# Decoder layer: project the raw transposed activations and apply the first layer norm to the products

## The reference, cut to what matters

```python
def _layernorm(x, axis=-1, eps=1e-05):
    m = jnp.mean(x, axis=axis, keepdims=True)
    v = jnp.var(x, axis=axis, keepdims=True)
    return (x - m) / jnp.sqrt(v + eps)

def _L0_attn_ref(x, Wqkv, bqkv, Wo, bo):          # d = 256
    qkv = jnp.einsum('bsc,cf->bsf', x, Wqkv) + bqkv
    q, k, v = ...
    attn = jax.nn.softmax(jnp.einsum('bqd,bkd->bqk', q, k) * scale, axis=-1)
    return jnp.einsum('bsd,dc->bsc', attn @ v, Wo) + bo

x = x + _L0_attn_ref(_layernorm(x), Wqkv, bqkv, Wo, bo)
x = x + fake_quant(_layernorm(x)) @ fake_quant(ctx)      # ctx (2, 1024, 1024)
x = x + _L0_ffn_ref(_layernorm(x), c1_w, c2_w, w1, w2t)  # picks 1 of 64 hidden units, 3584 in all
```

## Time and profile before

| | |
|---|---|
| median of 3 runs | 773.7 us (773.12 to 774.2) |
| the profiled execution | 773.81 us |
| its span in the profile | 772.0 us |
| instructions | 11300 |
| PE busy | 764.8 us, 99% |
| DVE busy | 606.9 us, 79% |
| POOL busy | 483.8 us, 63% |
| ACT busy | 242.4 us, 31% |

### The profile page before, as it was taken

One profiled execution on the slowest core, in us unless ns is written; L12 is line 12 of the kernel. 1 busy time (PEld: TensorE's weight loads), 2 busy tenths in 40 slices (PEclk: granted clock), 3 DMA queues, 4 the chain that ended last, 5 costly groups with the idle time before them and its releaser, 6 DMA issues.

```text
span 772.0 us, 11300 instructions
## 1 busy us (share of the span) xinstructions
PE 764.8 (99%) x3604; PEld 627.6 (81%) x3608; DVE 606.9 (79%) x963; ACT 242.4 (31%) x368; POOL 483.8 (63%) x306
## 2 busy tenths in 40 slices
PE   8999999999999999999999999999999999999998
PEld 7888887478888888888888888888888888888886
DVE  5887769997884878887878788788888887778864
ACT  5348668773321130312122221203031212222120
POOL 4887798766999974645636372636464563736360
PEclk9999999999999999999999999999999999999999
DMA  9436405400111121222222221212122222222114
GB/s 335 190 111 216 167 4 157 60 7 8 62 54 60 41 67 52 69 75 68 75 68 68 68 75 61 73 36 66 56 68 75 68 75 68 68 68 68 61 41 191
DMA packets 57319, 63.70 MB, mean 83 GB/s; under 512 B 39120, under 2 KB 41168, under 8 KB 57040
## 3 DMA queue, kind: packets, MB, share of 16 engines
q1 hardware_dynamic: 57152, 62.35, 25.9%
q10 hardware_dynamic: 144, 1.05, 0.3%
HBM read 50.79 MB, written 4.19 MB: 71 GB/s over the span
## 4 chain that ended last, share of the span: by engine, by line
PE 93%; DVE 4%; DMA 1%; ACT 1%; issue 1%; SPq 0%; DVEq 0%; ACTq 0%
PE bank L1881 13%; PE bank L1880 13%; PE bank L1882 13%; PE bank L1781 12%; PE bank L1782 12%; PE bank L1780 12%; PE bank L1589 4%; PE bank L1591 4%; PE bank L1590 4%; PE bank L1771 2%; DVE x L1267 1%; DMA x<-x_in 1%; PE bank L1750 1%; DVE xn L1248 1%; PE bank L1732 1%; PE bank L1605 1%
## 5 line engine op out<-in xcount | busy, mean ns | idle before, releaser
L1880 PE MATMUL bank<-w_hi,h_hi 128*128 128x512 f32 x448 | 175.2, 391 | 0.0
L1881 PE MATMUL bank<-w_lo,h_hi 128*128 128x512 f32 x448 | 175.0, 391 | 0.0
L1882 PE MATMUL bank<-w_hi,h_lo 128*128 128x512 f32 x448 | 174.3, 389 | 0.0
L1387 DVE TENSOR_TENSOR x<-bank,x 128x512 f32<-128x512 f32 x208 | 133.5, 685 | 48.9 <-PE bank L1882 48.8
L641 POOL TENSOR_TENSOR lo_r<-r,slot 128x512 fp32r<-128x512 f32 x52 | 68.1, 1311 | 141.0 <-ACT slot L880 141.0
L1882 PEld LDWEIGHTS bank<-w_hi,h_lo 128*128 128x128 f32 x448 | 84.1, 188 | 17.8
L1880 PEld LDWEIGHTS bank<-w_hi,h_hi 128*128 128x128 f32 x448 | 84.1, 188 | 17.2 <-POOL w_lo L646 0.2
L1881 PEld LDWEIGHTS bank<-w_lo,h_hi 128*128 128x128 f32 x448 | 84.4, 188 | 15.2
L1780 PE MATMUL bank<-xT_hi,slot 128*128 128x512 f32 x240 | 93.7, 390 | 0.0
L1781 PE MATMUL bank<-xT_lo,slot 128*128 128x512 f32 x240 | 93.4, 389 | 0.0
L1782 PE MATMUL bank<-xT_hi,lo_r 128*128 128x512 f32 x192 | 74.7, 389 | 0.0
(11 more groups left out here) (213 smaller groups left out, 1585.2 us busy)
## 6 DMA issues: line engine op xcount, KB each, us to landing
r<-w SPq DMA_DIRECT2D x56, 256.0 KB, 3.6
w_raw<-w SPq DMA_DIRECT2D x28, 512.0 KB, 4.0
x<-x_in SPq DMA_DIRECT2D x8, 512.0 KB, 10.3
ctx_raw<-ctx_in SPq DMA_DIRECT2D x8, 512.0 KB, 3.7
xn<-ctx_in SPq DMA_DIRECT2D x8, 512.0 KB, 4.3
out<-x SPq DMA_DIRECT2D x7, 512.0 KB, 2.6
W_raw<-wqkv SPq DMA_DIRECT2D x6, 512.0 KB, 11.0
xT_raw<-xT_in SPq DMA_DIRECT2D x1, 2048.0 KB, 19.8
```

Source lines behind the costliest of these rows:

```text
L1387: nc.vector.tensor_tensor(x[:, t, c], bank[unit_banks(g)[p]][:, :], x[:, t, c], ALU.add).then_inc(unit_added, 1)
L1880: nc.tensor.matmul(dst, h_hi[:, j, m], w2_hi[:, j, c], start=j == 0, stop=False)
L1881: nc.tensor.matmul(dst, h_hi[:, j, m], w2_lo[:, j, c], start=False, stop=False)
L1882: last = nc.tensor.matmul(dst, h_lo[:, j, m], w2_hi[:, j, c], start=False, stop=j == GJ - 1)
```

## The change

The raw transposed activations of both batches are loaded (xT_in is now of both), split and multiplied, and the norm is applied to the products. With r the scale and s the shift of a token, (x r + s) W = r (x W) + s (sum of W over channels). So:

- Q and K of batch 0 come first, as one product over eight slabs of 128 channels into four banks at once (`project_first_qk`), each chunk of one or two slabs as its loads land. The T1 jobs, the R jobs and ACT's norm of round 0 are gone. WARM is 18.
- DVE makes the lo part of the raw xT of batch 0 (`lo_xT0`, SBUF operands), POOL that of batch 1 (`lo_xT1`), and DVE sums the weight slabs one by one (`sum_W`, 7 steps of 512 columns, `sum_W_value`, 7 of 256). Each step waits for the one before. PE finishes the sum over partitions (`sum_weights`, within V(0,0)).
- PE spreads r and s of a batch into banks 7 and 6, ACT copies them to SBUF (`copy_rows`). DVE multiplies each Q bank by r (`scale_Q`) and adds s times the weight sum (`shift_Q`) before ACT's hi_Q. Each V half gets two steps of the same kind on DVE (`lo_V`) in the place of one addition for both.
- The loads are in another order, with one load issued by ACT. The first context load waits for V(0,1). POOL's add_bo runs behind the statistics of its tile and is spread among other work; the output bias has its own semaphore.

The diff, cut to its core:

```diff
-WARM = 44
+WARM = 18
+K_CHUNKS = [(0, 1), (1, 2), (2, 4), (4, 6), (6, 8)]
-    jobs = both("T1", 0) + both("T1", 1) + both("T1", 2) + [("V", 0, 0)] + both("T1", 3)
-    jobs += [("V", 0, 1), ("Q", 0, 0), ("R", 0), ("Q", 0, 1), ("R", 1), ("Q", 0, 2), ("Q", 0, 3), ("V", 1, 0)]
+    jobs = [("Q", 0, c) for c in range(4)] + [("V", 0, 0), ("V", 0, 1), ("V", 1, 0)]
...
 # SP
-            load_x(0, 1)
-            load_W(W_ORDER[0], 0, 1)
-            load_x(2, 3)
-            load_W(W_ORDER[1], 0, 1)
...
+            load_xT0(0)
+            load_xT0(1)
+            load_W(1)
+            load_xT0(2)
+            load_W(2)
+            load_x(0)
+            load_xT0(3)
+            load_W(3)
+            load_x(1)
+            load_xT0(4)
+            load_W(4)
+            load_x(2)
+            load_W(VALUE_CHUNK)
+            load_x(3)
+            load_W(VALUE_CHUNK + 1)
+            sp.dma_start(bqk_s[:, :], bqk).then_inc(bias_loaded, 16)
+            sp.dma_start(bv_b[:, :], bv.partition_broadcast(P)).then_inc(bias_loaded, 16)
+            load_xT1(0, 1)
+            sp.dma_start(bo_b[:, :], bo.partition_broadcast(P)).then_inc(bo_loaded, 16)
             load_x(4, 5)
+            load_xT1(2, 3)
...
+            load_x(6, 7)
-            sp.wait_ge(mm_done, nth("Q", 0, 3) + 1)
+            sp.wait_ge(mm_done, nth("V", 0, 1) + 1)
 # POOL
+            for c in range(VALUE_CHUNK + 2):
...
+                nc.gpsimd.tensor_tensor(w_part(W_lo, c), w_part(W_raw, c), w_part(W_hi, c).bitcast(F32),
+                                        ALU.subtract).then_inc(W_lo_done, 1)
+            lo_xT1(0, 1)
...
-            add_bo(0, 1, 2, 3)
-            lo_xT(0)
-            add_bo(4)
-            lo_xT(1)
-            add_bo(5)
+            add_bo(0)
+            lo_xT1(2, 3)
+            add_bo(1, 2, 3, 4)
             convert_ctx(0, 1)
+            add_bo(5)
+            convert_ctx(2, 3)
             add_bo(6)
-            convert_ctx(2, 3)
+            convert_ctx(4, 5)
             add_bo(7)
-            convert_ctx(4, 5, 6, 7)
+            convert_ctx(6, 7)
 # ACT
+            for c in range(VALUE_CHUNK):
+                hi_xT0(c)
+                if c > 0:
+                    hi_W(c)
+            hi_W(VALUE_CHUNK)
+            hi_W(VALUE_CHUNK + 1)
             roots(0, 0)
...
+            hi_xT1(0)
+            hi_W_ksum()
+            copy_rows(0)
+            for c in range(1, X1_CHUNKS):
+                hi_xT1(c)
+            for c in range(4):
+                hi_Q(0, c)
             hi_V(0, 0)
...
             hi_V(0, 1)
...
             scale_ctx(0)
             scale_ctx(1)
+            roots(0, 4)
...
+            copy_rows(1)
             for c in range(4):
                 hi_Q(1, c)
                 scale_ctx(2 * c + 7)
                 scale_ctx(2 * c + 8)
 # DVE
+            def scale_Q(b, c):
+                dve.wait_ge(mm_done, nth("Q", b, c) + 1)
+                dve.wait_ge(rows_copied, 2 * b + 1)
+                link(nc.vector.tensor_tensor(job_bank("Q", b, c)[:, :], job_bank("Q", b, c)[:, :], row_home[0][:, :],
+                                             ALU.mult))
+            def shift_Q(b, c):
+                dve.wait_ge(rows_copied, 2 * b + 2)
+                nc.vector.scalar_tensor_tensor(job_bank("Q", b, c)[:, :], row_home[1][:, :], wsum[:, c:c + 1],
+                                               job_bank("Q", b, c)[:, :], ALU.mult, ALU.add).then_inc(q_scaled, 1)
+            def add_slab(total, before, slab):
+                nc.vector.tensor_tensor(total, before, slab, ALU.add).then_inc(W_ksummed, 1)
+                ksums[0] += 1
+                dve.wait_ge(W_ksummed, ksums[0])
...
+            nc.vector.tensor_copy(w_part(W_hi, 0), w_part(W_raw, 0)).then_inc(W_hi0_done, 1)
+            lo_xT0(0)
+            lo_xT0(1)
+            sum_W(1)
+            lo_xT0(2)
+            sum_W(2, 3)
+            first_stats(0)
+            lo_xT0(3)
+            sum_W(4, 5)
+            first_stats(1)
+            lo_xT0(4)
+            sum_W(6, 7)
+            first_stats(2)
+            first_stats(3)
             norm_scale(0, 0)
...
+            sum_W_value(1, 2, 3)
+            sum_W_value(4, 5, 6, 7)
+            lo_W_ksum()
+            for c in range(4):
+                scale_Q(0, c)
+            copy_wsum()
+            shift_Q(0, 0)
+            shift_Q(0, 1)
             lo_Q(0, 0)
-            norm_xT(0)
+            shift_Q(0, 2)
             lo_Q(0, 1)
-            norm_xT(1)
+            shift_Q(0, 3)
             lo_Q(0, 2)
+            first_stats(4)
+            lo_Q(0, 3)
...
+            lo_V(0, 0)
+            first_stats(5)
+            lo_V(0, 1)
+            first_stats(6)
+            first_stats(7)
             round_ctx(0)
+            norm_scale(0, 4)
             round_ctx(1)
             lo_V(1, 0)
...
             for c in range(4):
+                scale_Q(1, c)
+                shift_Q(1, c)
                 lo_Q(1, c)
                 round_ctx(2 * c + 7)
                 round_ctx(2 * c + 8)
 # PE
-            transpose_norm(0, 0)
-            transpose_norm(0, 1)
-            first_values(lambda: transpose_norm(0, 2))
-            transpose_norm(0, 3)
+            project_first_qk()
+            spread_rows(0)
+            project_v(0, 0, sum_weights)
             project_v(0, 1)
-            project_qk(0, 0)
-            spread_rows(0)
...
             project_v(1, 0)
             for i in range(TB):
                 scores(0, i)
-            for c in range(4):
+            project_qk(1, 0)
+            spread_rows(1)
+            for c in range(1, 4):
                 project_qk(1, c)
             project_v(1, 1)
```

More of the change, by code:

```diff
@@ L136, in decoder_layer @@
     xT_lo = [at(f"xT_lo{b}", 48 + 32 * b, [P, KD, SB], F32R) for b in range(NB)]
-    xT_raw = at("xT_raw", 80, [P, KD, SB], F32)
+    xT_raw = [at(f"xT_raw{b}", 48 + 32 * b, [P, KD, SB], F32) for b in range(NB)]
     W_hi = at("W_hi", 96, [P, 3, KD, HD], F32R)
@@ L1052, in _ @@
             hi_u(0)
[L1053 to L1054 removed]
+            both(hi_T, 6)
+            both(hi_T, 7)
             hi_w2(0, 0)
@@ L1158, in lo_T, with lo_xT0 @@
                         xT_hi[t // TB][:, k, m].bitcast(F32), ALU.subtract))
-            def norm_xT(p):
-                dve.wait_ge(mm_done, nth("R", p) + 1)
-                dve.wait_ge(xT_loaded, 16)
-                row = job_bank("R", p)[:, :].rearrange("p (s o m) -> p s o m", s=2, o=1)
-                scale, shift = (row[:, s].to_broadcast([P, 4, 2 * P]) for s in range(2))
-                for h in range(2):
-                    part = xT_raw[token_pair(p, h)]
-                    link(nc.vector.tensor_tensor(part, part, scale, ALU.mult))
-                    last = nc.vector.tensor_tensor(part, part, shift, ALU.add)
-                    if h == 0:
-                        last.then_inc(xT_normed, 1)
-                free(last)
+            def lo_xT0(c):
+                dve.wait_ge(xT0_hi_done, c + 1)
+                k = chunk(c)
+                nc.vector.tensor_tensor(xT_lo[0][:, k, :], xT_raw[0][:, k, :], xT_hi[0][:, k, :].bitcast(F32),
+                                        ALU.subtract).then_inc(xT0_lo_done, 1)
@@ L1603, in transpose_norm @@
                         c = slice((4 * h + k) * P, (4 * h + k + 1) * P)
[L1604 to L1605 removed]
+                        last = nc.tensor.transpose(job_bank(*job)[:, k * P:(k + 1) * P], xn3[t % 4][:, c], id_f[:, :])
                     last.then_inc(mm_done, 1)
[L1608 to L1617 removed]
@@ new lines, in spread_rows, with project_first_qk, each @@
+            def spread_rows(b):
+                pe.wait_ge(rstd_ready, nth_chain(0, TB * b) + 1)
+                if b == 1:
+                    pe.wait_ge(rows_copied, 2)
+                for row, cols in zip(rows_bank, (rstd, nmr)):
+                    for i in range(TB):
+                        t = TB * b + i
+                        last = nc.tensor.transpose(row[:, i * P:(i + 1) * P], cols[:, t:t + 1].to_broadcast([P, P]), id_f[:, :])
+                last.then_inc(rows_spread, 1)
+            def project_first_qk():
+                for c, (first, stop) in enumerate(K_CHUNKS):
+                    for k in range(first, stop):
+                        def each(W, xT):
+                            for n in range(4):
+                                last = nc.tensor.matmul(job_bank("Q", 0, n)[:, :], W[:, n // DC, k, (n % DC) * P:(n % DC + 1) * P],
+                                                        xT[:, k, :], start=k == 0 and W is W_hi and xT is xT_hi[0],
+                                                        stop=k == KD - 1 and W is W_lo)
+                                if k == KD - 1 and W is W_lo:
+                                    last.then_inc(mm_done, 1)
+                        if k == first:
+                            pe.wait_ge(xT0_hi_done, c + 1)
+                            if c == 0:
+                                pe.wait_ge(W_hi0_done, 1)
```

(9 more changed lines are left out.)

401 lines of the change are left out of this document (182 added, 219 removed).

## The result

The changed kernel took 794.4, 794.6 and 798.2 us in three of its four runs; the fourth (1984.8) was disturbed and counts in the median on record, 796.4, but in no comparison. The kernel before took 773.5 on the same chip: ratio 1.029, 95% interval 1.0274 to 1.0306. The profiled execution took 794.39 with a span of 792.6; before, 773.81 and 772.0. The forecast was 792.

A forecast was written before the change was run, and what follows sets the result against it. PE bounds the kernel before; in the changed head DVE, held by POOL, would. PE's 7.5 us gain is lost and scores of batch 1 end 18.4 later: 773.8 + 18.4 = 792.2, say 792; forecast 787 to 796, range 779 to 799.

The forecast's parts named there:

- PE's gain of 7.5: Head of the kernel: PE's shorter list would end V(1,1) at 81.6 instead of 89.07, if only PE mattered.
- DVE's chain: From 39.6: DVE sets the pace, first remainder of batch 1 ends at 86.5, then 5.76 us per chunk.
- The exclusion: First stretch: DVE's two-SBUF-operand operations and POOL's run one at a time; slab sums held three times for 2.3 to 2.4.
- the 27.4 and 31.4: First stretch: excluded DVE work and POOL's weight splits need 27.4 us one at a time, from 4.0 to 31.4 at best.
- the qd group: DVE's one-column operations on qd and qp, after 39.6: 5.5 us, with three waits on POOL.
- The end of the scores: Batch 1: scores wait for lo_Q(1,3) and lo_V(1,1) and end at 114.7 instead of 96.3, 18.4 later.
- rival 4: Holes of 4.2, 5.3 and 5.4 in PE's list let its clock fall, giving 797; 12%.
- Nothing given back behind: Behind the scores of batch 1: same list on a full PE, so the 18.4 us loss stays.
- 1: Head: PE stays the bound and DVE keeps ahead, giving 766; 4%.
- 2: Head: the exclusion hardly costs in the new order, scores end at 94.7, giving 772; 7%.
- 3: First stretch: only its two-operand operations go free, W_ksum 9 us sooner, giving 783.5; 14%.
- 5: Whole change: it does nothing, gain and holds cancel; 2%.

The follow-up runs named there:

- e5: The changed kernel with the running sum of the Q and K slabs in a PSUM bank instead of SBUF; 4.3 us earlier by the ratio, 5.0 by the span.
- e4: The changed kernel with 44 warm-up transposes in place of 18; 1.9 us slower by the ratio, 4.0 by the span.
- e6: The changed kernel with dummy transposes where PE stands idle before row spreading and the scores of batch 1; 1.4 us earlier by the ratio.
- e13: Combined version, same result as the changed kernel: one-column operations at DVE's start, Q and K sums in PSUM, dummy transposes; ratio 1.0092 to the kernel before.

## Why the prediction was right

The mechanism was right, the end of the scores was missed by 1.9 us through a term left out of the sum, and two parts of the sum came out by luck. The three undisturbed runs lie at 794.4 to 798.2; of them 798.2 is above the forecast's own 787 to 796, all are within 779 to 799. Step by step, in its own order:

- **PE's gain of 7.5.** The list got shorter, and PE stood idle 3.1 and 1.7 us before the row spreading and the weight sums (forecast 4.2 and 2.8). V(1,0) ended at 56.5, 1.9 behind the forecast, which DVE's chain hid; 1.0 of it arose at the start, where the 18 warm-up transposes ended at 5.6 and not at 4.6.
- **The exclusion.** Three pairs of slab sums were held, at 10.76, 18.90 and 25.66, for some 2.3 each (forecast at 15.4, 22.7 and 25.7, for 2.3 to 2.4). Holds that the list of three lacks are those of the first sum (1.78 in all) and of xT_lo at 15.73 (3.25) and 23.87 (1.87). Yet rstd and nmr were done at 33.67 (33.0) and W_ksum was split by 40.73 (39.6): the total came nearer than its parts, which is luck. By its own terms the excluded work is 12.3 us (4.8, 6.6 and 0.9), not 13, so the 27.4 and 31.4 should be 26.7 and 30.7; no later term of the forecast uses them. e5 shows the cause, not only the coincidence.
- **DVE's chain.** First remainder ended at 86.26 (86.5), fourth at 103.34 (103.8), v_lo(1,1) at 109.68 (110.5); spacing 5.7 (5.76). Under this lies a second piece of luck: the qd group was held twice, not three times as I wrote, and took 4.9 us from its first start to its last end against 5.5; e4 shows that it can as well be held four times, 4.6 more. 798.2 among the runs may be such an execution, which no trace of it shows.
- **The end of the scores.** 114.7 forecast, 116.6 seen. From the end of v_lo(1,1) it took 6.9 us where the forecast had 4.2; the 0.8 by which v_lo(1,1) came early hides a part. The missing 2.7 are the clock: I gave it as rival 4 and left it out of the sum. After the 5.15 us hole the granted clock fell to 0.50, the 1.2 GHz level, and the score products came 0.43 apart in place of 0.23; the first six of them ran into the second hole, which was 3.35 and not 5.4 in part for that, and twelve behind it, 2.5 us, lay on PE's path. It is a term besides the holds, not one in their place; e6 shows it by the clock and the count of products.
- **Nothing given back behind.** From the scores on 676.0 us against 675.9. POOL's sums ended 2.1 later than forecast, with the scores.
- **Rivals.** 1 and 2 fell with the first remainder at 86.26 and the scores at 116.6. 3 fell too: slab sums of the first stretch were held, and W_ksum was split at 40.73 and not 9 us sooner. 4 holds for its cause, at about half its price (2.6 us where it had 5). 5 fell.

## What to carry to other kernels

Before giving an engine's idle time to new work, ask whether that work can run beside what its neighbours do then: here 6.6 us (an estimate) of sums with two SBUF operands took 17.3, for they waited for POOL, and with the Q and K total in PSUM in place of SBUF they took 12.2. Look for the shortest operations too: four of one column cost 0.6 or 9.3 us, by what POOL had started just before. And where a hole is put into TensorE's list, add what the slower clock takes from the work behind it.

## What the runs showed of the hardware

- Whether a one-column DVE operation with two SBUF operands takes 0.14 or 2.4 us turned on 0.03 to 0.04 us of order against POOL; kernels that differ elsewhere moved by up to 4.6 us through it.
- A sum over elements 1 KB apart in SBUF read 1024 of them in 2.0 us, unhindered by POOL; an addition of 512 columns with one operand in PSUM took 0.7.
- Four half-kilobyte loads issued behind one of 256 KB at the start took 6.0 to 8.6 us to land (e13), when all loads together ran at 239 GB/s (5 to 10 us).
- After PE had stood still for 5.15 us the granted clock was 0.50 (the 1.2 GHz level) and products of 512 columns came 0.43 us apart in place of 0.23; with dummy transposes in the holes (e6) it stayed at 1.00.
